# Decoder layer with routed experts, last stage: the second scaling handed from VectorE to ScalarE and TensorE, and the last pair normalised ahead of the others

## The reference, cut to what matters

```python
        tgt2 = jnp.einsum('bsed,bse->bsd', o, router_w)
        return _layer_norm(tgt + tgt2, gamma, beta)      # (x - mu) * rsqrt(var + eps) * gamma + beta
    ...
    x = _layernorm(x + _L0_ffn_ref(x, ...), axis=-1)     # (x - mean) / sqrt(var + eps)
```

## Time and profile before

| what | us |
|---|---|
| median of 3 runs (lowest, highest) | 209.13 (209.09, 209.26) |
| the profiled execution, its own time | 208.87 |
| its span, first to last instruction | 207.0 |
| TensorE busy in the span | 176.3 |
| VectorE busy | 154.9 |
| ScalarE busy | 117.1 |
| GpSimd busy | 60.7 |
| mean granted TensorE clock, share of full | 0.969 |

### The profile page before, as it was taken

One profiled execution on the slowest core, in us unless ns is written; L12 is line 12 of the kernel. 1 busy time (PEld: TensorE's weight loads), 2 busy tenths in 40 slices (PEclk: granted clock), 3 DMA queues, 4 the chain that ended last, 5 costly groups with the idle time before them and its releaser, 6 DMA issues.

```text
span 207.0 us, 4786 instructions
## 1 busy us (share of the span) xinstructions
PE 176.3 (85%) x1735; PEld 129.2 (62%) x1735; DVE 154.9 (75%) x396; ACT 117.1 (57%) x245; POOL 60.7 (29%) x76
## 2 busy tenths in 40 slices
PE   7999999979799977899999779678699999998400
PEld 6554556554253746475575577567699999996300
DVE  1579999998989677468668778865676888654891
ACT  2189979602464415337788388267256777641544
POOL 4000000000040000005398378976045555550000
PEclk9999999999999999999999999889999999999965
DMA  5999999998999296979829613013234100005011
GB/s 135 320 190 260 216 267 211 299 418 334 240 299 268 70 321 145 313 178 341 286 68 314 206 24 127 26 34 91 56 80 104 52 22 25 19 0 158 0 46 44
DMA packets 13467, 34.20 MB, mean 165 GB/s; under 512 B 2096, under 2 KB 5606, under 8 KB 13443
## 3 DMA queue, kind: packets, MB, share of 16 engines
q1 hardware_dynamic: 12356, 32.27, 55.6%
q0 software_dynamic: 1088, 1.62, 2.5%
HBM read 28.01 MB, written 6.38 MB: 166 GB/s over the span
## 4 chain that ended last, share of the span: by engine, by line
PE 52%; DVE 18%; issue 10%; POOL 8%; DMA 5%; ACT 3%; DVEq 1%; SPq 0%; POOLq 0%; ACTq 0%
PE bank L538 9%; PE bank L485 9%; POOL ret L1817 8%; PE bank L561 6%; PE bank L504 5%; PE bank L495 5%; PE bank L548 5%; PE bank L473 3%; DMA xpad<-x_T 3%; DVE ph L1459 2%; DMA ctxT_slot<-ret 2%; DVE neg_max L1355 2%; DVE xtok L1688 1%; PE bank L801 1%; DVE sel L1394 1%
## 5 line engine op out<-in xcount | busy, mean ns | idle before, releaser
L1601 DVE SCALAR_TENSOR_TENSOR ctx_slot<-bank,ctx_slot 128x512 f16<-128x512 f32 (+1 forms) x28 | 18.7, 672 | 13.6 <-ACT ctx_slot L1074 8.6
L1817 POOL DMA_INDIRECT ret<-ctx_slot,ctxT_slot x20 | 19.6, 980 | 21.5 <-ACT ctx_slot L1087 19.6
L1074 ACT ACTIVATE ctx_slot<-bank 128x512 f16<-128x512 f32 (+1 forms) x28 | 16.2, 581 | 16.3 <-PE bank L762 16.3
L538 PE MATMUL bank<-ctxT_slot,w_conv 97*64 97x500 f32 x96 | 21.8, 589 | 2.4 <-ACT pc L921 1.4
L473 PE MATMUL bank<-reset 128*128 128x224 f32 x62 | 18.1, 438 | 1.4 <-DVE reset L1134 1.4
L485 PE MATMUL bank<-xpad,w_conv 128*128 128x448 f32 x48 | 18.3, 539 | 0.0
L1758 POOL TENSOR_TENSOR home<-home 128x896 f32<-128x896 f32 x1 | 2.1, 2081 | 55.2 <-ACT home L877 55.2
L561 PE MATMUL bank<-ctx_slot,ph 125*64 125x96 f32 (+1 forms) x384 | 17.6, 248 | 0.5 <-DVE res L1465 0.4
L561 PEld LDWEIGHTS bank<-ctx_slot,ph 125*64 125x64 f32 (+1 forms) x384 | 16.1, 133 | 2.2 <-DVE res L1465 1.0
L1355 DVE TENSOR_REDUCE neg_max<-bank 120x1 f32<-120x1500 f32 x8 | 13.7, 1716 | 4.3 <-PE bank L538 4.2
L473 PEld LDWEIGHTS bank<-reset 128*128 128x128 f32 x62 | 14.0, 240 | 3.2 <-DVE reset L1134 1.4
(11 more groups left out here) (219 smaller groups left out, 421.6 us busy)
## 6 DMA issues: line engine op xcount, KB each, us to landing
ctx_slot<-ctx SPq DMA_DIRECT2D x16, 576.0 KB, 5.8
ctxT_slot<-ctx_T SPq DMA_DIRECT2D x16, 562.5 KB, 10.8
w_raw<-w SPq DMA_DIRECT2D x16, 256.0 KB, 7.8
slots<-w_raw SPq DMA_DIRECT2D x4, 910.0 KB, 28.4
ctxT_slot<-slots SPq DMA_DIRECT2D x20, 65.0 KB, 1.9
convw_sb<-conv_w SPq DMA_DIRECT2D x3, 256.0 KB, 6.7
ctxT_slot<-ret SPq DMA_DIRECT2D x3, 224.0 KB, 3.8
small_sb<-small SPq DMA_DIRECT2D x1, 526.0 KB, 11.1
```

Source lines behind the costliest of these rows:

```text
L538: mm = pe.matmul(bank[j * GAP:j * GAP + rows, n, 0:SN], qk_all[:, at:at + rows], ctxT_slot[:, s, j, n * SN:(n + 1) * SN], start=True, stop ...
L1074: nc.scalar.activation(hh[:, n % 3, :, 0:cols], bank[:, n % 3, :].rearrange("p (f t) -> p f t", f=FC) [:, :, 0:cols], ACT.Relu).then_inc(t ...
L1601: V.scalar_tensor_tensor(hl[:, n % 3, :, 0:cols], bank[:, n % 3, :].rearrange("p (f t) -> p f t", f=FC) [:, :, 0:cols], 0.0, hh[:, n % 3, ...
L1817: G.indirect_dma_start(ret[:], bass.IndirectOffsetOnAxis(ap=xs_u[:, t, D + 1:D + 2], axis=0), out_st[:, t % OB, :], None, bounds_check=2 * ...
```

## The change

Quarters 0 to 3 now cover pairs 0 to 6 alone (quarter 3 is pair 6), and pair 7 is a group of its own, counted as group 0 of `f_var`, `f_rstd`, `f_var2`, `f_rstd2`, ahead of the quarters.

- VectorE: `last_pair()` runs both norms' statistics, the centring and the sum for pair 7 before the first quarter's outs are back. In a quarter, the multiplication with rstd and the addition of x2 + beta (L1688) are gone; it waits for `f_sum` and takes the second statistics from PSUM. For pair 7 and quarters 2 and 3 it does the last scaling itself (`vector_final`, a `tensor_scalar`); `final_bias` stays for quarters 0 and 1.
- ScalarE: new `scaled(q)`, which multiplies the centred rows with rstd in place (Copy with a scale of one value a partition); `final_norm` for quarters 0 and 1 alone, and from PSUM.
- TensorE: two more matmuls against the identity a quarter (`with_x2`), x2b and the scaled rows, into other banks. It waits ahead of the first addition for `t_acc` and `m_x2b`.
- SyncE: five stores in place of four: pair 7, then quarters 0 to 3.

```diff
--- before.py
+++ after.py
@@ -345,7 +345,8 @@
         m_x2b = sem("x2_plus_beta_ready")
         f_var, f_rstd = sem("first_variance_ready"), sem("first_rstd_ready")
         f_var2, f_rstd2 = sem("last_variance_ready"), sem("last_rstd_ready")
-        f_bias, f_out = sem("final_bias_ready"), sem("final_ready")
+        f_bias, f_out, f_outv = sem("final_bias_ready"), sem("final_ready"), sem("vector_final_ready")
+        f_cent, f_scaled, f_sum = sem("first_centred"), sem("first_scaled"), sem("first_sum_done")
         s_store = sem("stored")
 
         block = stack.enter_context(nc.Block())
@@ -358,6 +359,8 @@
         X1_PARTS = (range(0, 1), range(1, PPH), range(PPH, PAIRS))
         T_BANK, QK_BANK = (4, 3, 7), (6, 5, 7)
         SUM_BANK, TURN_BANK = 5, 6
+
+        SUM_AT, NORM_AT = (3, 7, 0, 1), (2, 5, 6, 4)
 
         def pairs_done(n):
 
@@ -457,11 +460,13 @@
             for q in range(4):
                 w = slice(2 * q, min(2 * q + 2, XP))
                 sp_.dma_start(got[:, w], ret.rearrange("(p i w) d -> p i w d", p=PT, i=XP)[:, w]).then_inc(g_ld[q], 16)
-            for q in range(4):
-                sp_.wait_ge(f_out, q + 1)
-                w = slice(2 * q, 2 * q + 2)
+            for n, w in enumerate((slice(XP, PAIRS), slice(0, 2), slice(2, 4), slice(4, 6), slice(6, XP))):
+                if n in (1, 2):
+                    sp_.wait_ge(f_out, n)
+                else:
+                    sp_.wait_ge(f_outv, n - 1 if n else 1)
                 sp_.dma_start(out[:, w, :], x1[:, w, :]).then_inc(s_store, 16)
-            sp_.wait_ge(s_store, 16 * 4)
+            sp_.wait_ge(s_store, 16 * 5)
 
 
         @block.tensor
@@ -795,18 +800,34 @@
                 outs(n)
 
 
-            SUM_AT = (3, 7, 0, 1)
-
-            def summed(q, rows_, width, start=False, stop=False):
-                return pe.matmul(bank[0:PT, SUM_AT[q], 0:width], ident[0:PT, 0:PT], rows_, start=start, stop=stop)
+            def added(to, rows_, start=False, stop=False):
+                width = rows_.shape[1] * D
+                return pe.matmul(bank[0:PT, to, 0:width], ident[0:PT, 0:PT], rows_, start=start, stop=stop)
+
+            def returns(q):
+                w = slice(2 * q, min(2 * q + 2, XP))
+                added(SUM_AT[q], x2[:, w, :], start=True)
+                pe.wait_ge(g_ld[q], 16)
+                added(SUM_AT[q], got[:, w, 0, :])
+                added(SUM_AT[q], got[:, w, 1, :], stop=True).then_inc(f_y, 1)
+
+            def with_x2(q):
+                w = slice(2 * q, min(2 * q + 2, XP))
+                added(NORM_AT[q], x2b[:, w, :], start=True)
+                pe.wait_ge(f_scaled, q + 1)
+                added(NORM_AT[q], acc[:, w, :], stop=True).then_inc(f_sum, 1)
 
             pe.wait_ge(t_hl, len(SEQUENCE))
-            for q in range(4):
-                w = slice(2 * q, min(2 * q + 2, XP))
-                summed(q, x2[:, w, :], (w.stop - w.start) * D, start=True)
-                pe.wait_ge(g_ld[q], 16)
-                summed(q, got[:, w, 0, :], (w.stop - w.start) * D)
-                summed(q, got[:, w, 1, :], (w.stop - w.start) * D, stop=True).then_inc(f_y, 1)
+            pe.wait_ge(t_acc, E)
+            pe.wait_ge(m_x2b, PAIRS)
+            returns(0)
+            returns(1)
+            returns(2)
+            with_x2(0)
+            returns(3)
+            with_x2(1)
+            with_x2(2)
+            with_x2(3)
 
 
         @block.scalar
@@ -1100,31 +1121,43 @@
                     weighted(n)
 
 
-            def final_inv_std(q, second):
-                w = slice(2 * q, 2 * q + 2)
-                act.wait_ge(f_var2 if second else f_var, q + 1)
+            def final_inv_std(n, second):
+
+                w = slice(XP, PAIRS) if n == 0 else slice(2 * n - 2, min(2 * n, XP))
+                act.wait_ge(f_var2 if second else f_var, n + 1)
                 inv_std(own, mv[:, w, 1], lnv[:, w], rstd2[:, w] if second else rstd[:, w],
                         f_rstd2 if second else f_rstd)
+
+            def scaled(q):
+                act.wait_ge(f_cent, q + 1)
+                act.wait_ge(f_rstd, q + 2)
+                for j in range(2 * q, min(2 * q + 2, XP)):
+                    ins = nc.scalar.activation(acc[:, j, :], acc[:, j, :], ACT.Copy, scale=rstd[:, j:j + 1])
+                ins.then_inc(f_scaled, 1)
 
             def final_norm(q):
                 act.wait_ge(f_bias, q + 1)
                 for j in (2 * q, 2 * q + 1):
-                    ins = nc.scalar.activation(x1[:, j, :], acc[:, j, :], ACT.Identity, bias=nmr[:, j:j + 1],
-                                               scale=rstd2[:, j:j + 1])
+                    ins = nc.scalar.activation(x1[:, j, :], bank[0:PT, NORM_AT[q], (j % 2) * D:(j % 2 + 1) * D],
+                                               ACT.Identity, bias=nmr[:, j:j + 1], scale=rstd2[:, j:j + 1])
                 ins.then_inc(f_out, 1)
 
             final_inv_std(0, False)
+            final_inv_std(0, True)
             final_inv_std(1, False)
-            final_inv_std(0, True)
+            scaled(0)
             final_inv_std(2, False)
-            final_norm(0)
+            scaled(1)
             final_inv_std(1, True)
             final_inv_std(3, False)
+            scaled(2)
+            final_norm(0)
+            final_inv_std(2, True)
+            final_inv_std(4, False)
+            scaled(3)
             final_norm(1)
-            final_inv_std(2, True)
-            final_norm(2)
             final_inv_std(3, True)
-            final_norm(3)
+            final_inv_std(4, True)
 
 
         @block.vector
@@ -1657,62 +1690,80 @@
                     staged(n - (HEAD + E - 3))
 
 
-            def summed_at(j):
-
-                if j == XP:
-                    return acc[:, j, :]
-                return bank[0:PT, (3, 7, 0, 1)[j // 2], (j % 2) * D:(j % 2 + 1) * D]
+            def moments(n, at, done):
+
+                pairs = range(XP, PAIRS) if n == 0 else range(2 * n - 2, min(2 * n, XP))
+                for j in pairs:
+                    a = own.mark(V.bn_stats(stat[:, j, :], at(j)))
+                own.need(a)
+                for j in pairs:
+                    a = V.bn_aggr(mv[:, j, :], stat[:, j, :])
+                a.then_inc(done, 1)
+
+            def returned_at(j):
+                return bank[0:PT, SUM_AT[j // 2], (j % 2) * D:(j % 2 + 1) * D]
+
+            def normed_at(j):
+                return bank[0:PT, NORM_AT[j // 2], (j % 2) * D:(j % 2 + 1) * D]
+
+            def last_pair():
+
+                j = XP
+                dve.wait_ge(t_acc, E)
+                dve.wait_ge(m_x2b, PAIRS)
+                moments(0, lambda j: acc[:, j, :], f_var)
+                dve.wait_ge(f_var, 1)
+                a = own.mark(V.scalar_tensor_tensor(acc[:, j, :], acc[:, j, :], mv[:, j, 0:1], par("gamma", PT),
+                                                    ALU.subtract, ALU.mult))
+                own.need(a)
+                dve.wait_ge(f_rstd, 1)
+                a = own.mark(V.scalar_tensor_tensor(acc[:, j, :], acc[:, j, :], rstd[:, j:j + 1], x2b[:, j, :],
+                                                    ALU.mult, ALU.add))
+                own.need(a)
+                moments(0, lambda j: acc[:, j, :], f_var2)
 
             def returned(q):
 
                 dve.wait_ge(f_y, q + 1)
-                if q == 3:
-                    dve.wait_ge(t_acc, E)
-                for j in (2 * q, 2 * q + 1):
-                    a = own.mark(V.bn_stats(stat[:, j, :], summed_at(j)))
-                own.need(a)
-                for j in (2 * q, 2 * q + 1):
-                    a = V.bn_aggr(mv[:, j, :], stat[:, j, :])
-                a.then_inc(f_var, 1)
-
-            def last_sum(q):
-
-                dve.wait_ge(m_x2b, PAIRS)
-                dve.wait_ge(f_var, q + 1)
-                for j in (2 * q, 2 * q + 1):
-                    a = own.mark(V.scalar_tensor_tensor(acc[:, j, :], summed_at(j), mv[:, j, 0:1], par("gamma", PT),
-                                                        ALU.subtract, ALU.mult))
-                own.need(a)
-                dve.wait_ge(f_rstd, q + 1)
-                for j in (2 * q, 2 * q + 1):
-                    a = own.mark(V.scalar_tensor_tensor(acc[:, j, :], acc[:, j, :], rstd[:, j:j + 1], x2b[:, j, :],
-                                                        ALU.mult, ALU.add))
-                own.need(a)
-                for j in (2 * q, 2 * q + 1):
-                    a = own.mark(V.bn_stats(stat[:, j, :], acc[:, j, :]))
-                own.need(a)
-                for j in (2 * q, 2 * q + 1):
-                    a = V.bn_aggr(mv[:, j, :], stat[:, j, :])
-                a.then_inc(f_var2, 1)
+                moments(q + 1, returned_at, f_var)
+                dve.wait_ge(f_var, q + 2)
+                for j in range(2 * q, min(2 * q + 2, XP)):
+                    ins = V.scalar_tensor_tensor(acc[:, j, :], returned_at(j), mv[:, j, 0:1], par("gamma", PT),
```

(30 more changed lines are left out.)

## The result

| | before | changed |
|---|---|---|
| median (lowest, highest) | 209.19 us (208.84, 209.44), 6 runs | 206.27 us (205.15, 210.24), 6 runs |
| profiled execution: its time, its span | 208.87, 207.0 | 205.54, 203.7 |

The ratio is 0.985, with a 95% interval of 0.9805 to 0.9895: 3.1 us faster, between 2.2 and 4.1. The ratios here leave out runs that a lower clock had disturbed, the medians don't. The same code gave 0.9878 (0.9839 to 0.9917) and 0.9879 (0.9826 to 0.9932) in two later comparisons, which is 2.6 and 2.5 us of the times beside them. The forecast was 205.7 by the median and 205.44 for the profiled execution, which took 205.54. So all three ratios give less than the forecast gain of 3.43 us, but their intervals reach 4.1, 3.5 and 3.6 us and take it in.

What follows compares the result with a forecast made beforehand. VectorE was taken to set the pace for 10 us at the end; the step-by-step new order ended the span at 203.57 instead of 207.0, a 3.43 us gain, so 209.13 - 3.43 = 205.70 us, range 204.9 to 206.9.

Steps and rivals of the forecast that it cites:

- Part 1: VectorE before the first quarter: pair 7's work needs 1.94 of 2.07 us idle time and fits with 0.1 to spare.
- TensorE's new waits: Ahead of TensorE's first addition: they move it from 188.21 to 188.79 and cost nothing, with 0.2 of cover.
- Part 2: Middle quarters: VectorE idles 0.45 us for TensorE before summed(0), from 193.84 to 194.29; returned(2) ends at 196.40.
- Part 3: The end: ScalarE takes over the pace, its quarter 2 rstd ends at 200.32, vector_final(4) at 201.26, span at 203.57.
- rival 1: Chain between engines costs more than summed, including late matmuls at half clock: gain 2.6 us, 206.5; chance 0.25.
- rival 5: VectorE's last scalings slower from PSUM: vector_final(3) takes 0.76, time 205.8; chance 0.12.
- VectorE's own work without any wait: About 9.9 us from 190.84, so perfect ordering gives only 0.5 more and the range's lower end lies near 204.9.
- signs of being wrong: Next profile: returned(0) after 190.84, VectorE waiting for TensorE in quarters 2 or 3, or slower scaled, vector_final or last landing.
- rival 4: ScalarE: Copy between Ln and Exp forces table loads, 1.28 us each, up to 213.4; chance 0.04, shared with other losses.
- Rival 3: VectorE stays the bound and the change frees nothing; 3 us given back, 208.7; chance 0.05.
- Rival 2: Pair 7 overruns its hole on VectorE; past 0.45 more it costs one for one, 206.2 at 1 us; chance 0.04.

Runs made afterwards that it cites:

- early_add: TensorE's two waits moved from ahead of its first addition to ahead of the first that needs them, against the changed kernel; ratio to before 0.9818.
- one_store: Stores of quarters 2 and 3 in one of 168 KB after VectorE's last instruction, against the changed kernel; ratio to before 0.9905.
- after_third: The changed kernel profiled a third time, with no edit; ratio to before 0.9879.
- pair6_on_vector: Pair 6's product with rstd and addition of x2 + beta put back on VectorE, against the changed kernel; ratio to before 0.9886.
- Combined: Pair 6 on VectorE, TensorE's waits moved back, and late steps reordered on VectorE and ScalarE, against the changed kernel; ratio to before 0.9817.
- hand_over_only: The changed kernel without pair 7 moved forward: quarter 3 has pairs 6 and 7, four stores; ratio to before 0.9948.

## Why the prediction was right, step by step

**The bound before, and the size.** VectorE set the pace, and taking work off it was worth what the sum said: A shrank by 3.43, forecast 3.43. Experiments with one part alone gave 2.20 and 1.38. The mechanism was right; that the size met the forecast so closely was luck, as this table shows. Its times count from TensorE's first addition of outs (189.68 in the forecast, 189.81 measured).

| | forecast, us | measured, us |
|---|---|---|
| ScalarE's last rstd of quarter 2 is there | 10.64 | 10.46 |
| VectorE's last scalings begin | 10.67 | 10.60 |
| they end | 11.58 | 11.69 |
| the span ends | 13.89 | 13.89 |

**Part 1, pair 7 in the hole.** It was right that the work is hidden, and wrong that it fits. From 188.87 + 0.35 = 189.22 it took until 191.32, 2.10 in place of 1.94, since each met wait cost 0.04 and not 0.03, and the sum started 0.11 after its rstd. In this execution the last pair step on VectorE also ended 0.46 later than before, while the additions of the outs began only 0.13 later, so the first statistics started 0.4 after the sums were there. As written, TensorE's chain had room for it: VectorE's wait before the second statistics of quarter 0 shrank from the forecast 0.45 to 0.11. Where the load came later (early_add, one_store) the wait was 0.45 and 0.44. TensorE's new waits were costed at nothing with 0.2 of cover. Here the cover was gone: no wait for the load is in sight, and the outs' additions start when the first one lets them. As VectorE waited only 0.11 for TensorE before those second statistics, these waits can't have cost the stage more than that.

**Part 2.** From the first addition of outs to the sum of quarter 0 it was 4.57 by the forecast and 194.29 - 189.81 = 4.48 in the profile.

**Part 3.** ScalarE's last rstd of quarter 2 was forecast for 200.32 and came at 200.27, in a stage that had begun 0.13 later. Inside that, `scaled` was 0.394 and 0.69 a pair (0.37 and 0.66 taken), and `final_norm` from PSUM 0.79 a pair (0.86 taken): terms of opposite sign. The last matmul was longer than summed: 0.72 at a granted clock falling to 0.50, in place of 0.38. That is rival 1's mechanism, priced there at 0.1. It kept VectorE at pair 6's statistics, so that its last scalings start at 200.41, 0.14 after ScalarE's rstd in place of 0.03. In after_third, where the same matmul took 0.47, they start 0.04 after it, and B is 0.13 shorter. The three last scalings took 1.09 together in place of 0.91: rival 5's mechanism, real but small. The tail after the last instruction was 2.20; the forecast had 201.26 to 203.57, 2.31. Of the terms on the path at the end, the one most off is thus `vector_final`, by 0.18.
The Trainium skill (VectorE: DVE Perf Modes, The perf-mode tier table) gave an estimated 0.07 us more from PSUM for each of them; pair6_on_vector has both forms, 0.402 from the bank and 0.342 from SBUF, 0.06 apart, so the trace agrees.
The Trainium skill (ScalarE: Activation LUTs, What ACT_TABLE_LOAD costs) gave an estimated 0.386 for `scaled`; the trace has 0.394.

**The range.** Its lower end rested on a wrong sum. VectorE's own work without any wait was put at 9.9 us; the prediction's own terms add up to about 9.0, and the profile has VectorE busy 8.55 of the 10.26 us from its first statistics of quarter 0 to its last instruction. Combined has the same stretch in 9.36, although VectorE does pair 6's product and sum in it, and counted from the first addition of outs VectorE is done 0.65 earlier than in the changed kernel. So the 0.5 us named there was not the limit.

**The signs.** As forecast, ScalarE had no gap over 0.1 from 196.45 to 200.27, and the last two stores went out near 201. But two signs of being wrong showed with the gain unharmed: the first statistics of quarter 0 came at 191.24, and VectorE waited 0.84 for TensorE before the last statistics. The second was no good sign, as the prediction's own times had a wait there, from about 199.2 to 199.59.

**Rivals.** No table load appears in the stage (rival 4). Rival 3 falls with hand_over_only. Rival 2's overrun happened and was taken up by TensorE's chain, whose room was 0.45.

**The median.** 206.27 against 205.70: three of the six runs took 207.0, 207.2 and 210.2. The profiled execution took 205.54 against 205.44. Why executions differ ahead of the stage wasn't studied.

## What to carry to other kernels

Where one engine paces a chain of small tiles, count what leaves it and then lay out the new order on every engine, instruction by instruction. The busy times of the whole span don't show such a gain (VectorE 154.9 to 153.9 us), as most of what left the stage moved ahead of it or to other engines. In the stage they do: from the first statistics of quarter 0 to VectorE's last instruction its busy time went from 10.57 to 8.55 us. Handing an operation over pays while the giving engine has other tiles to work on; for the last single tile the trip over two engines cost 0.5 us more than doing it in place. A hole ahead of a stage can be filled to the brim if the next thing on the path has slack, and it is worth finding that slack first.

## What the runs showed that was not expected

The granted clock after sparse matmuls differs between executions of one program: 0.65 in 199 to 200 us of the first profile, with the last matmul at 0.72 us, and 1.00 in the same microsecond of after_third, with 0.47 us for the same matmul, at the same distance from the ones ahead of it (1.12 us idle both times).
A scaling on ScalarE with both pointers took 0.442 us from PSUM and 0.482 from SBUF. The Trainium skill (VectorE: DVE Perf Modes, The TRN2 errata) has ScalarE 52 cycles of 1.2 GHz cheaper from PSUM, an estimated 0.043 us; the trace agrees with 0.040 here. Between the product on ScalarE (0.394 from SBUF) and the same function from PSUM (0.368) it is 0.026. The prediction should have used it.
